# Expert loads behind the value products, and a new order of the last pass, in an AdaLN block with retention attention and a top-2 MoE

## The reference, cut to what matters

```python
x = L0_attn_x                                    # 4 x 512 x 256, fp32
h = layernorm(x) * (1 + ca) + sa
q, k, v = (h @ w + b for q, k, v)                # 16 heads of 16
scores = (q k^T) * gamma^(n-m), n >= m           # retention, no softmax
ret = scores @ v ; norm = groupnorm(ret) over (d) per head, then over n
x = x + ga * (silu(h @ wg + bg) * norm @ wo + bo)
h = layernorm(x) * (1 + cb) + sb
logits = h @ gate ; top 2 of 8 experts, softmax of the two
x = x + gb * sum_e combine_e * (silu(h @ w0[e]) * (h @ w1[e])) @ wo[e]    # 256 -> 512 -> 256
```

## Time and profile before

| what | us |
|---|---|
| median of 3 runs (430.96, 423.73, 430.70) | 430.7 |
| the profiled execution | 425.93 |
| its span | 424.1 |
| TensorE busy in the span | 366.8 (86%) |
| DVE busy | 261.6 (62%) |
| POOL busy | 228.5 (54%) |
| ACT busy | 168.5 (40%) |
| mean granted TensorE clock | 0.952 |

### The profile page before, as it was taken

One profiled execution on the slowest core, in us unless ns is written; L12 is line 12 of the kernel. 1 busy time (PEld: TensorE's weight loads), 2 busy tenths in 40 slices (PEclk: granted clock), 3 DMA queues, 4 the chain that ended last, 5 costly groups with the idle time before them and its releaser, 6 DMA issues.

```text
span 424.1 us, 11477 instructions
## 1 busy us (share of the span) xinstructions
PE 366.8 (86%) x3889; PEld 273.3 (64%) x3890; DVE 261.6 (62%) x726; ACT 168.5 (40%) x258; POOL 228.5 (54%) x172
## 2 busy tenths in 40 slices
PE   3897899899898754799979399999999999999980
PEld 3475467767765553465745268888888888888860
DVE  6358348557736873663775147777777777777740
ACT  3424344636442120314112215555555555555520
POOL 3102610917842733271446716777777777777751
PEclk9998999999989967899989869999999999999996
DMA  6819251394565612177357514433333333333322
GB/s 224 274 24 321 106 203 49 69 307 166 161 172 189 226 54 77 45 259 114 75 147 233 147 55 75 77 75 75 75 75 75 75 75 75 75 75 75 51 25 25
DMA packets 34050, 50.62 MB, mean 119 GB/s; under 512 B 3390, under 2 KB 20700, under 8 KB 34012
## 3 DMA queue, kind: packets, MB, share of 16 engines
q1 hardware_dynamic: 25384, 36.17, 29.6%
q0 software_dynamic: 8176, 13.65, 14.5%
q10 hardware_dynamic: 452, 0.28, 0.2%
HBM read 31.92 MB, written 18.16 MB: 118 GB/s over the span
## 4 chain that ended last, share of the span: by engine, by line
PE 67%; DVE 10%; DMA 9%; issue 5%; POOL 3%; ACT 3%; POOLq 1%; ACTq 1%; DVEq 0%; SPq 0%
PE ps L1668 14%; PE ps L1375 11%; PE ps L1649 6%; PE ps L1648 6%; PE ps L1652 6%; PE ps L1394 3%; PE ps L1464 3%; PE ps L1660 3%; DMA out_dram<-wg_s,qd 3%; DVE sm L999 3%; POOL routed L581 3%; PE ps L1489 3%; PE ps L1639 2%; DMA routed<-h,idx 2%; PE ps L1557 2%
## 5 line engine op out<-in xcount | busy, mean ns | idle before, releaser
L612 POOL TENSOR_TENSOR w_lo<-we,w_hi 128x1024 fp32r<-128x1024 f32 x30 | 74.0, 2466 | 27.1 <-ACT w_hi L789 27.1
L1668 PE MATMUL ps<-we,qeo 128*128 x312 | 76.5, 389 | 1.5 <-ACT qeo L774 1.1
L1668 PEld LDWEIGHTS ps<-we,qeo 128*128 128x128 f32 x312 | 58.1, 192 | 20.3 <-issue 12.8
L774 ACT COPY qeo<-ps 128x512 f32<-128x512 f32 x39 | 22.9, 587 | 117.2 <-PE ps L1660 117.2
L622 POOL DMA_INDIRECT out_dram<-wg_s,qd x30 | 46.8, 1559 | 35.3 <-DMA out_dram<-wg_s,qd 14.2
L1278 DVE TENSOR_TENSOR w_halves<-we,w_halves 128x1024 fp32r<-128x1024 f32 x30 | 36.8, 1225 | 7.1 <-ACT w_halves L789 7.0
L1250 DVE CAST rT_halves<-ps 128x256 fp32r<-128x256 f32 x30 | 12.7, 425 | 42.3 <-PE ps L1557 42.3
L581 POOL DMA_INDIRECT routed<-h,idx x32 | 32.7, 1023 | 10.3 <-issue 9.0
L1639 PE MATMUL ps<-we,xn 128*128 x72 | 36.7, 635 | 0.0
L789 ACT CAST w_halves<-we 128x1024 fp32r x30 | 31.5, 1049 | 0.4 <-issue 0.4
L789 ACT CAST w_hi<-we 128x1024 fp32r x30 | 31.6, 1053 | 0.0
(11 more groups left out here) (224 smaller groups left out, 714.2 us busy)
## 6 DMA issues: line engine op xcount, KB each, us to landing
rowbuf<-routed SPq DMA_DIRECT2D x39, 260.5 KB, 2.9
we<-in_ffn_w_kernel_dram SPq DMA_DIRECT2D x16, 512.0 KB, 5.8
we<-in_ffn_wo_kernel_dram SPq DMA_DIRECT2D x8, 512.0 KB, 7.7
routed<-z SPq DMA_DIRECT2D x9, 260.5 KB, 2.6
xs<-in_attn_x_dram SPq DMA_DIRECT2D x4, 512.0 KB, 12.1
out_dram<-xs SPq DMA_DIRECT2D x4, 512.0 KB, 4.3
h<-gb_dram SPq DMA_DIRECT2D x16, 128.0 KB, 5.7
we<-in_wmod_dram SPq DMA_DIRECT2D x1, 1024.0 KB, 10.2
```

Source lines behind the costliest of these rows:

```text
L612: g.tensor_tensor(w_lo[1], expert_up(e, 1), w_hi[1].bitcast(F32), ALU.subtract)\
L1668: last = mm(down_ps, eit[s % 2][:, k, :], weights(e, 2 * FT * F + k * D, D), start=k == 0, stop=k == KF - 1)
```

## The change

- SP: from pass 1 on both experts are loaded together when `values(p, 1)` is through (`pv_done`), not at the q and k products. The store of batch `p - 1`, `load_ga`, `load_sbcb(p)` and `fill_gb(p)` then wait for the gate product (`g1`, or `g0` in the last pass). Stores come one pass later.
- `fill_gb` is one transfer into block 0 of `h2`; a new ACT copy, `gb_copies`, of 128x768 elements spreads it to the other three blocks, and the scatter waits for that copy (`gb_copied`) where it waited for the transfers.
- Tiles 0 and 1 are loaded without a wait for `row_used`; `store_x(2)` and `load_sbcb(3)` follow tile 1's load, `store_x(3)` tile 3's.
- The first table: `places(1)` and `rows_of_tokens(1)` go ahead of the group statistics, `counts` right behind `values(2, 1)`, `firsts` behind the rows of k, `fold` behind the scores of half 0. On DVE `tile_columns(0)` stands ahead of the states, `table_rows(0)`, the gate and the masks of half 0 ahead of `attention_out(2)`.
- The end of the first part: `values(3, 0)`, `turn_h2(2)`, `values(3, 1)`, `turn_rows(0)`, the last gate product, `average(3)`, `router(2)`, `average_dev(3)`, `pe_step(0)` with `rank(2)` ahead of its end, `out_rows(3)`. The choice of experts for batch 2 and its `places` move behind batch 3's group statistics on DVE; `group_normed(3)` and `gb_copies(2)` go ahead of ACT's first tile.
- POOL: `scatter(2)` is split in halves around `second_scale(3)`; `modulate(3)` comes after `add_rows(1)` and not 2; the halves of `scatter(3)` come after `add_rows(2)` and `add_rows(3)`, not 4 and 5.
- Batch 3's choice comes after `hidden(3)`, `rank(3)` one place later in step 4, and `table_rows(1)` inside step 7.
- Batch 2's `h2T` takes `kT`'s memory; in the setup `turn_x(0)` goes ahead of the turn of the small vectors.

```diff
             items.append((b - 2, "logits", "dve"))
-        if b >= 2:
+        if 2 <= b < B:
             items.append((b - 2, "rank", "dve"))
+        if b == B - 1:
+            items.append((b, "counts", "dve"))
+        if b == B:
+            items.append((b - 2, "logits", "dve"))
         if b >= 1:
             items.append((b - 1, "gn", "dve"))
+        if b == B:
+            items.append((b - 2, "rank", "dve"))
+        if b == B - 1:
+            items.append((b, "firsts", "dve"))
         if b < B:
             items += [(b, "stE", "dve"), (b, "stO", "dve")]
+        if b == B - 1:
+            items.append((b, "fold", "dve"))
         if b >= 1:
             items += [(b - 1, n, "dve") for n in ("wo01", "wo23")]
-        if b == B - 1:
-            items += [(b, n, "dve") for n in ("counts", "firsts", "fold")]
-        if b >= 1:
             items += [(b - 1, "h2T0", "act"), (b - 1, "h2T1", "act")]
-        if b >= B - 1:
-            items.append((b - 1, "logits", "dve"))
-    return items + [(B - 1, "rank", "dve")]
+    return items + [(B - 1, "logits", "dve"), (B - 1, "rank", "dve")]
...
-        h2T = [qd, qd, qd, hT]
+        h2T = [qd, qd, kT, hT]
         st1 = st2
...
-        c_in, wmod_in, wmod_late, vec_in, gam_in, bv_in, bo_in, w_in, wg_in, wo_in, we_in, gb_rows = sems(
-            "c_in wmod_in wmod_late vec_in gam_in bv_in bo_in w_in wg_in wo_in we_in gb_rows")
+        c_in, wmod_in, wmod_late, vec_in, gam_in, bv_in, bo_in, w_in, wg_in, wo_in, we_in, gb_rows, gb_copied = sems(
+            "c_in wmod_in wmod_late vec_in gam_in bv_in bo_in w_in wg_in wo_in we_in gb_rows gb_copied")
         ga_in, sbcb_in = sems("ga_in0 ga_in1"), sem("sbcb_in")
...
                     sp.wait_ge(scattered, SCATTERS * b)
-                for t in range(NC):
-                    sp.dma_start(h2[:, t, GB:ROW], gb_dram[b].partition_broadcast(P)).then_inc(gb_rows, 16)
+                sp.dma_start(h2[:, 0, GB:ROW], gb_dram[b].partition_broadcast(P)).then_inc(gb_rows, 16)
...
                 p = b - 1
-                sp.wait_ge(front.full, front.filled(b, "q0"))
+                if b == 0:
+                    sp.wait_ge(front.full, front.filled(b, "q0"))
+                else:
+                    sp.wait_ge(pv_done, SETS * b)
                 if b == B - 1:
...
                 load_expert(2 * b)
-                sp.wait_ge(front.full, front.filled(b, "k0"))
                 load_expert(2 * b + 1)
                 if p >= 0:
-                    store_x(p, x2_out)
+                    sp.wait_ge(front.full, front.filled(b, "g0" if b == B - 1 else "g1"))
+                    if p >= 1:
+                        store_x(p - 1, x2_out)
                     if b + 1 < B:
...
                         load_ga(b + 1)
+                    if p >= 1:
+                        sp.wait_ge(h2_ready, p)
+                        load_sbcb(p)
                     fill_gb(p)
-                    if b < B - 1:
-                        sp.wait_ge(h2_ready, b)
-                        load_sbcb(b)
...
                 r = sp.value_load(table(i)[0:1, 0, bass.ds(i, 1)], min_val=0, max_val=PAD_ROW)
-                sp.wait_ge(row_used, i + 1)
+                if not (isinstance(i, int) and i < 2):
+                    sp.wait_ge(row_used, i - 1)
                 sp.dma_start(rows[s % 2], routed[bass.ds(r, P), :]).then_inc(row_in[s % 2], 16)
...
                 load_rows(i, i)
-                if i == 0:
+                if i == 1:
+                    store_x(B - 2, x2_out)
                     sp.wait_ge(h2_ready, B - 1)
                     load_sbcb(B - 1)
-                if i == 2:
+                if i == 3:
                     store_x(B - 1, x2_last)
...
                 if 0 in tiles:
-                    settle(pool, [(idx_ready, b + 1), (row_ready, b + 1), (gb_rows, 16 * NC * (b + 1)),
+                    settle(pool, [(idx_ready, b + 1), (row_ready, b + 1), (gb_copied, b + 1),
                                   (h2_ready, b + 1)], pool_passed)
...
             group_power(B - 1)
-            scatter(B - 2, range(NC))
+            scatter(B - 2, (0, 1))
             second_scale(B - 1)
+            scatter(B - 2, (2, 3))
...
                 add_rows(i, i, first=i == 0)
-                if i == 2:
+                if i == 1:
                     modulate(B - 1)
-                if i in (4, 5):
-                    scatter(B - 1, (2 * i - 8, 2 * i - 7))
+                if i in (2, 3):
+                    scatter(B - 1, (2 * i - 4, 2 * i - 3))
                 if i == EARLY - 4:
...
+
+            def gb_copies(b):
+                act.wait_ge(gb_rows, 16 * (b + 1))
+                a.copy(h2[:, 1:NC, GB:ROW], h2[:, 0:1, GB:ROW].broadcast_to([P, NC - 1, D])).then_inc(gb_copied, 1)
...
                 keys(b, 1)
+                if p >= 1:
+                    gb_copies(p - 1)
                 if p >= 0:
...
                     h2_features(p)
-                    if final:
-                        top_tanh(p)
             b = B - 1
             gate(b, 1)
+            top_tanh(b - 1)
+            group_normed(b)
+            gb_copies(b - 1)
             act.sem_inc(it_act, 1)
...
             act_step(0, 0)
-            group_normed(b)
             act_step(1, 1)
...
             top_tanh(b)
+            gb_copies(b)
             run_steps(act, act_step, first=4)
...
                 if p >= 0:
-                    group_stats(p)
                     if p >= 1:
                         places(p - 1)
-                    group_center(p)
-                    if p >= 1:
                         rows_of_tokens(p - 1)
...
                         tiles_of_experts(0)
+                        tiles_before(0)
+                    group_stats(p)
+                    group_center(p)
                     group_variance(p)
...
                     first_stats(1)
+                if last:
+                    tile_columns(0)
                 states(b)
...
                     first_stats(2)
+                if last:
+                    table_rows(0)
                 gates(b, 0)
+                if last:
+                    masks(b, 0)
                 if p >= 0:
                     attention_out(p)
-                if last:
-                    tiles_before(0)
-                masks(b, 0)
-                if last:
-                    tile_columns(0)
-                    table_rows(0)
-                else:
+                if not last:
+                    masks(b, 0)
                     gates(b, 1)
...
                 masks(b, 1)
-                if last:
-                    take_logits(p)
-                    choose_top(p)
-                    choose_places(p)
-                    choose_weights(p)
...
-            def dve_step(i, s, hidden_made=False):
+            def dve_step(i, s, hidden_made=False, between=None):
                 const = isinstance(i, int)
...
                     weighted(i - 2, s - 2)
+                if between is not None:
+                    between()
                 if not (const and not 0 <= i + 1 < N_TILES):
...
             b = B - 1
-            dve.sem_inc(row_used, 2)
             dve.sem_inc(in_done, 4)
...
+            group_stats(b)
             take_rows(0, 0)
-            group_stats(b)
             group_center(b)
-            places(b - 1)
             gates(b, 1)
+            take_logits(b - 1)
+            choose_top(b - 1)
             group_variance(b)
-            rows_of_tokens(b - 1)
+            choose_places(b - 1)
             group_scale(b)
+            choose_weights(b - 1)
             take_rows(1, 1)
...
             hidden(0, 0)
+            places(b - 1)
+            rows_of_tokens(b - 1)
             attention_out(b)
...
             hidden(1, 1)
-            for i in range(2, 8):
-                dve_step(i, i, hidden_made=i == 2)
-                if i == 3:
-                    take_logits(b)
-                    choose_top(b)
-                    choose_places(b)
-                    choose_weights(b)
-                elif i == 4:
-                    places(b)
-                    rows_of_tokens(b)
-                    tiles_of_experts(1)
-                elif i == 5:
-                    tiles_before(1)
-                elif i == 6:
-                    tile_columns(1)
-                elif i == 7:
-                    table_rows(1)
+            dve_step(2, 2, hidden_made=True)
+            dve_step(3, 3)
+            hidden(3, 3)
+            take_logits(b)
+            choose_top(b)
+            choose_places(b)
+            choose_weights(b)
+            dve_step(4, 4, hidden_made=True)
+            places(b)
+            rows_of_tokens(b)
+            tiles_of_experts(1)
+            dve_step(5, 5)
+            tiles_before(1)
+            dve_step(6, 6)
+            tile_columns(1)
+            dve_step(7, 7, between=lambda: table_rows(1))
             run_steps(dve, dve_step, first=8)
...
             mod_columns(ps[5], 1, 1).then_inc(setup_pe, 1)
```

(39 more changed lines are left out.)

## The result

| | median us | lowest to highest | runs |
|---|---|---|---|
| before | 429.60 | 423.73 to 430.96 | 4 |
| after | 418.91 | 412.50 to 424.81 | 4 |

The ratio is 0.966, with a 95% interval of 0.960 to 0.973: faster, by 10.7 us in the medians. Medians count all runs, ratios and their intervals only those within 1.5% of the kernel's fastest, which here are 412.50 and 415.67 against all four of before. The forecast was 413, range 404 to 426.

What follows compares the result with a forecast made beforehand. TensorE bounds the untouched expert loop from about 250 us; gains come from waits before it. Terms 0.8 + 0 + 0 + 4.5 - 0.8 + 7.75 + 2.7 = 14.9 us off 425.9 give 411.0; forecast 413, range 404 to 426.

Steps and rivals of the forecast that it cites:

- the 411.0: Whole kernel: forecast time in us, the profiled execution's 425.9 less the summed gain of 14.9.
- 14.9: Whole kernel: total gain in us, summed as 0.8 + 0 + 0 + 4.5 - 0.8 + 7.75 + 2.7.
- 4.5 - 0.8 + 7.75 + 2.7: Steps 4 to tile 9: unheld DVE operations 4.5, gb copy and DVE under `modulate(3)` -0.8, tile 9's wait 7.75, half clock 2.7.
- tile 9 waits again: Rival, chance 0.18: last scatter or table slips, the 7.75 us wait at tile 9's rows is only renamed; some 424.
- 171.3 - 136.26: Last pass, gate product 0 to `out_rows(3)`: `out_rows(3)` starts at 171.3 instead of 180.77, gain 9.5 us.
- 13.7: `turn_rows(0)` to `out_rows(3)`: 12.4 us, less 1.8 half clock, plus 1.7 `router(2)`, plus 1.4 tanh and gb copy.
- 192.7 - 171.3: `out_rows(3)` to `down(1)`: batch 2's scatter holds `down(1)` until 192.7, TensorE waits 7 us; 2.0 us left, half clock takes them.
- Loads, stores, gb at 0: Moved loads, stores and gb transfers: no net gain or loss, bounds -1.5 to +1.4 us.
- slower rival: Chance 0.07: expert loads make five small-product groups wait 1.36 us in each of three passes, 20.4 us lost; 434 to 436.
- the place that I had named: Last pass, where values waited on "issue": `counts(0)` waits there for `tiles_of_experts`; within the -1.5 to +1.4 us bounds.
- Setup 0.8: Setup: `turn_x(0)` no longer stands behind a waiting transpose, gain 0.8 us, bounds 0 to 0.9.
- The lock does move: Rival, chance 0.12: POOL operations from 152.7 to 162.1 hold DVE's `group_center` and choice for batch 2; some 417.

Runs made afterwards that it cites:

- 3: The kernel before with only the expert loads moved behind the values of each pass: 430.97 us, ratio 1.009.
- 4: The kernel before with only the `row_used` wait of tiles 0 and 1's loads removed: 427.81 us, ratio 1.002.
- 10: The kernel before with only POOL's new order of `modulate(3)` and the halves of `scatter(3)`: 425.36 us, ratio 0.978.
- 11: The kernel before with POOL's new order and no `row_used` wait for tiles 0 and 1: 420.31 us, ratio 0.971.
- 9: The changed kernel again, unedited, in the third job: 421.17 us for 432.98 before, ratio 0.975.
- 5: The changed kernel with store, ga, sbcb and gb back behind the second output product, pass 3's store behind tiles 0 and 1's loads: 421.70 us, ratio 0.977.
- 8: The changed kernel with POOL's old order of `modulate(3)` and the halves of `scatter(3)`: 434.49 us, ratio 1.006.
- 12: The changed kernel with group moved back, expert loads later and spread, batch 2's places sooner, padding and two stores behind later tiles: 420.65 us, ratio 0.973.
- 1: The changed kernel again, unedited, in the first job: 423.97 us for 433.59 before, ratio 0.990.
- 2: The changed kernel with the expert loads back at the q and k products: 420.76 us, ratio 0.977.
- 7: The changed kernel with batch 2's rank, places and rows of tokens sooner: 425.24 us, ratio 0.973.
- 6: The kernel before with pass 0's second expert loaded after the last scores, not the k product: 431.30 us, ratio 0.999.

## Why the prediction was right, and where not

Starts of four products show where the time goes, better than the totals do. From the turning of tile 10's rows to the end of the span it is 170.8 to 171.4 us in every row here: the loop is the same.

| kernel | last pass, gate product 0 | `out_rows(3)` | `down(1)` | rows of tile 10 | span |
|---|---|---|---|---|---|
| before, first profile | 136.26 | 180.77 | 194.70 | 253.05 | 424.1 |
| 3, loads moved | 141.76 | 185.73 | 200.86 | 258.24 | 429.0 |
| 4, rows | 142.80 | 183.08 | 197.06 | 253.61 | 424.4 |
| 10, POOL | 141.74 | 186.53 | 201.65 | 251.78 | 422.9 |
| 11, POOL and rows | 142.04 | 182.13 | 196.25 | 245.08 | 416.1 |
| after, first profile | 146.94 | 184.79 | 203.80 | 251.95 | 423.1 |
| 9, after | 144.66 | 182.88 | 202.16 | 250.25 | 421.6 |
| 5, group back | 141.09 | 176.86 | 197.04 | 249.24 | 420.6 |
| 8, old POOL order | 139.51 | 179.97 | 199.01 | 258.49 | 429.5 |

**What carries the gain.** Take the stretch from gate product 0 to the rows of tile 10. It is 116.8 us in before and 116.5 in kernel 3; 110.8 with the rows alone (4), 110.0 with POOL's order alone (10), 103.0 with both (11). The whole change has 105.0 and 105.6 (after, 9), and without POOL's order 119.0 (8). So the two small edits add up, 6 and 7 us, and the rest of the change taken together wins nothing here: beside kernel 11 it costs 2.0 and 2.6 us.

**The base.** The profile of before that I worked from reached the gate product 5.5 us sooner than kernels 3, 10 and 11, which have the same work up to there but for the loads. Its pass 0 has no "issue" wait; theirs have 2.9 to 3.9 us. I took its 425.93 as an ordinary execution with an offset of up to 4.8; it was a lucky one, of a kind that the changed kernel has too (kernels 5 and 8 show no such wait either). So the 411.0 was low from the start: 14.9 off the median of 429.6 would have been 414.7.

**From `down(1)` to tile 10: right.** I expected 4.5 - 0.8 + 7.75 + 2.7 = 14.15 us here. Measured, 58.35 (253.05 - 194.70) became 48.15, so 10.2. The turned rows of tiles 4, 7 and 8 cut it in pieces. From tile 4 to 7 it took 25.6 us and takes 21.2: 4.4 won, forecast 3.7. From 8 to 10 it took 22.1 and takes 11.35: 10.8 won, forecast 10.45. The two other pieces lose. From `down(1)` to tile 4 it is 2.6 us more, the half clock: 6.20 us of work at 0.56 is 6.20 x (1 - 0.56) = 2.7 too much. I had booked 2.0 of that to the stretch ahead. From tile 7 to 8 it is 2.4 more, which I had at nothing: 1.34 for the rows of tile 8 and 0.48 + 0.27 for a late table, since DVE's copy at 235.16 waits 2.30 us for POOL, whose adding of tiles now stands behind the scatters. That this gain is POOL's order is shown: without it the stretch is 59.5 us (kernel 8), with it alone 50.1 (kernel 10). The rival "tile 9 waits again" did not come true in the change; in kernel 12 it did, but not by the rival's road, since the last scatter was issued at 226.18, long before (rows at 241.12).

**From gate product to `out_rows(3)`: right in kind.** Before 44.5 us, after 37.9 and 38.2. I had forecast 171.3 - 136.26 = 35.0, so 9.5 us won; it was 6.6. The rows wait is the main part: kernel 11, with it alone, has 40.1 for kernel 10's 44.8. I had `turn_h2(2)` wait 3 us for ACT; it waited 0.21, since TensorE was itself late, by the 4.37 us on "issue" and the half clock behind it (5.46 us for 16 products that take 3.69 at full clock, as at 184.79). From `turn_rows(0)` to `out_rows(3)` it was 12.3 us, I had said 13.7, and I had added it up from TensorE's own work. That was the wrong engine: in the eight traces with the new order this piece takes 12.0 to 12.5 us, while TensorE's wait in it runs from 1.2 to 3.6. It is the chain of batch 3's group norm, over DVE, POOL and ACT, up to `gated(3)`.

**From `out_rows(3)` to `down(1)`: right.** The scatter of batch 2 is the next bound, as I wrote: wait 5.42 us (forecast about 7), half clock behind, 19.0 us for the stretch where before had 13.9 and I had worked out 192.7 - 171.3 = 21.4. So 6.6 us are won ahead of `out_rows(3)` and 5.1 given back; about 1.6 are left, forecast 2.0. Both parts were forecast too large, and it is partly luck that they cancel so well. Kernel 11, with the old order, wins 4.7 there (44.8 to 40.1) and gives nothing back (15.1 to 14.1). This is why it is as fast.

**Loads, stores, gb at 0: the step that failed.** I bounded it by -1.5 and +1.4 us. Pass 2, from its first q product to that of the last pass, took 38.5 to 40.9 us in the six traces with the group at its new place (after, kernels 1, 2, 7, 8 and 9), and 34.6 to 36.0 in the six kernels without the change (before, 3, 4, 6, 10 and 11); with the group back it took 36.1 and 35.9 (kernels 5 and 12). That is 3 us or more in this pass alone, and the wait at the scores of the last pass (3.3 to 4.5 us, 1.8 with the group back) comes on top. The step argued over the moved expert loads and said of the rest only that its users come late: it asked who waits for the data, and not what else needs the DMAs at that moment. My slower rival had the kind of wait, instructions that come late, but named the six expert loads; kernels 2 and 3 clear them for passes 2 and 3. Its price of 20.4 us, five groups in each pass, was far too high: all in all two groups wait longer than before, one in pass 2 and one in the last. `counts(0)` ahead of the gate product waits 1.24 us besides, at the place that I had named.

**The small terms.** Setup 0.8 expected and measured. The copy of gb takes 0.82 to 0.84 us, 0.8 expected. The table's column fell from 2.40 to 0.47 us. The 0.8 us of the setup are seen at `turn_x(0)` only; the first q product starts at 13.3 to 13.6 us in the eight traces with the change and at 13.4 to 14.5 in the six without. The lock does move, as the rival said, but to one copy on DVE, 1.47 us where it takes 0.29 elsewhere (174.50 above), and no wait is seen to hang on it.

**The sum.** 14.9 us forecast against 10.7, 9.6 and 11.8 by the medians of three jobs. The 3 to 5 us missing are of the size of pass 2's late instructions (3 us or more) and the late table and rows of tile 8 (2.4). From gate product 0 to tile 10 the two first profiles differ by 11.8 us, forecast 14.1. For a pair that had the wait of pass 0 both times, 9 and 3, the stretches add up: +2.90 - 5.75 + 4.15 - 9.29 = -7.99 us, which is 258.24 - 250.25.

**A wait that the profile does not name.** `out_rows(3)` waits 1.2 to 3.6 us on "issue" in every kernel, the one before too. In each of the fourteen traces it starts 0.10 or 0.11 us after the last operation of `gated(3)` on DVE has ended (184.69 and 184.79 above; 180.67 and 180.77 in before), and the kernel has it wait for just that. So this wait is for DVE, and no late instruction.

**Left open.** What decides whether pass 0 has its wait. And no kernel beat the changed one by more than the runs scatter: kernel 11 with the group norm chain and the scatter of batch 2 made shorter was not tried.

## What to carry to other kernels

Ask of a moved transfer not only who needs its data but which engine runs many short instructions while it fills the DMAs. On an engine with a queue of waiting work, the order alone can be worth more than a rebuilt schedule: here two edits of a few lines, one on POOL and one wait of SP, carry the effect of the whole change. And take the stretches between fixed instructions over several executions before a total is trusted; the profile to argue from may be a lucky one. Before a stretch is added up from one engine's work, look at which engine's result ends it: a wait marked "issue" may still be for another engine.

## What the runs showed of the hardware

Apart from the one before `out_rows(3)`, the long waits on "issue" stand at fixed products, whatever their length: 50 products before the end of `from_states` in pass 0 (43.46, and 41.21 in kernel 6), 52 in pass 2, 3 before the end of the scores in the last pass. The kernel has no wait between these products, since each group waits only ahead of its first. From the wait at 167.87 to the one at 171.48 TensorE runs 72 + 8 + 48 = 128 products, each with a weight load, so 256 instructions; from 156.85 to 167.87 it is 3 + 2 + 16 + 112 + 64 + 56 = 253 products, nearly twice that. A queue that brings instructions stands in the DMA list of the page of after, with 0.43 MB in 26 packets, or 16.5 KB each:

```profile
q8 instruction: 26, 0.43, 0.4%
```

The Trainium skill (Runtime: NRT & Kernel Launch, section "Instruction fetch mechanics") says that each engine's instruction memory is refilled in blocks of 256 instructions over a DMA queue of its own. The trace agrees, by the 128 products. It also says that the fetch is mostly hidden. Here, if these are fetches, it is not: 112 such products pass in 1.5 to 1.9 us at full clock, and beside full DMAs the wait was 2.5 to 4.5 us, with the clock at half behind it. That it falls with the transfers beside it is shown for pass 2 (3.41 to 0.69 us in kernel 5, 0.52 in kernel 12); in pass 0 it fell from 3 to 4 us to 0.91 in kernel 6, but was missing in three unedited traces too. That it is the fetch that waits is argued from place and spacing, not shown.
